# Moving two weight products ahead of the mask pooling in an eight-core masked linear and gated LoRA layer

## The reference

```python
xn = layernorm(x)
block_mask = mask.reshape(128, 32, 128, 32).sum(axis=(1, 3)) > 0      # 32 x 32 blocks of the int32 mask
s = einsum('bsk,nk->bsn', xn, weight * repeat(block_mask))            # 4096 x 4096
y = einsum('bth,oh->bto', xn, W_base) + b_base
z = einsum('bth,erh->bter', xn, lora_A[active])
alpha = softmax(log(domain_prior[active] + 1e-12) + logits(xn)[..., active])
y = y + einsum('bteo,bte->bto', einsum('bter,eor->bteo', z, lora_B[active]) * 2.0, alpha)
out = x + s * silu(y)
```

## Time and profile before

| | us |
|---|---|
| median of 3 runs | 2528.36 |
| lowest and highest run | 2517.14, 2659.54 |
| profiled execution, device time | 2527.91 |
| its span, slowest core (core 2) | 2526.2 |
| spans of the eight cores | 2501.1 to 2526.2 |
| iterations 0 to 20 of pass 0 | 367.4 to 1057.3 |
| iterations 21 to 31 of pass 0 | 1057.3 to 1366 |
| iterations of pass 1 | 1614 to 2520 |

### The profile page before, as it was taken

The page is one execution under the profiler, slowest core; times in us unless marked ns, Lnnn a source line. Parts: engine busy times, 40 slices in busy tenths (PEclk is TensorE's granted clock), DMA queues, the critical chain, the costliest instruction groups (busy, mean ns, idle before and its releaser), DMA issues.

```text
span 2526.2 us, 25213 instructions; the slowest of 8 cores (2501.1 to 2526.2 us)
## 1 busy us (share of the span) xinstructions
PE 2089.2 (83%) x8955; PEld 882.1 (35%) x8955; DVE 797.6 (32%) x871; ACT 469.2 (19%) x551; POOL 336.0 (13%) x260
## 2 busy tenths in 40 slices
PE   1135369889899898899998645699999999999998
PEld 0001024334344343344443101244444444444443
DVE  3631742444443344412221036322222122222221
ACT  2022001122111211222121320112211221122111
POOL 0123001111010111111012620010101010101010
PEclk9985579999999899999999556799999999999999
DMA  6853145667777676656563530256645665565552
GB/s 192 245 163 120 34 132 169 218 210 238 230 221 231 211 233 223 226 151 191 168 193 111 167 112 11 89 174 206 200 170 171 209 199 172 175 210 194 171 171 96
DMA packets 122834, 442.42 MB, mean 175 GB/s; under 512 B 15013, under 2 KB 15062, under 8 KB 122710
## 3 DMA queue, kind: packets, MB, share of 16 engines
q1 hardware_dynamic: 67414, 239.46, 30.2%
q10 hardware_dynamic: 46080, 167.79, 21.6%
q0 software_dynamic: 9216, 33.56, 3.3%
HBM read 407.17 MB, written 33.59 MB: 174 GB/s over the span
## 4 chain that ended last, share of the span: by engine, by line
PE 64%; DMA 16%; DVE 10%; issue 4%; POOL 3%; ACT 2%; SPq 1%; DVEq 0%; ACTq 0%; POOLq 0%
PE pb L741 30%; PE pb L761 29%; DMA mstage<-mkp 10%; DMA xbuf<-xt 3%; POOL sq L543 2%; DVE txn L612 2%; DVE xn L616 2%; DVE mcB L406 2%; DMA wstage<-wp 1%; DVE wm L498 1%; SPq L284 1%; PE pb L769 1%; DVE pooled L416 1%; PE pb L633 1%; DMA scr<-bm01a 1%
## 5 line engine op out<-in xcount | busy, mean ns | idle before, releaser
L741 PE MATMUL pb<-xn,wm 128*128 128x512 bf16 x4096 | 931.6, 387 | 48.1 <-DVE bm01a L435 48.1
L761 PE MATMUL pb<-xn,wb 128*128 128x512 bf16 x4096 | 904.9, 379 | 0.0
L741 PEld LDWEIGHTS pb<-xn,wm 128*128 128x128 bf16 x4096 | 405.5, 99 | 552.5 <-issue 89.9
L761 PEld LDWEIGHTS pb<-xn,wb 128*128 128x128 bf16 x4096 | 400.7, 98 | 483.4
L498 DVE TENSOR_TENSOR wm<-wstage,bmtexp 128x1024 bf16<-128x1024 f32 x256 | 342.8, 1339 | 646.4 <-DMA wstage<-wp 641.0
L797 POOL TENSOR_TENSOR out_sb<-sg_sb,xbuf 128x512 f32<-128x512 f32 x128 | 178.1, 1391 | 1932.2 <-DVE sg_sb L791 1932.2
L507 ACT CAST wb<-wbstage 128x1024 bf16<-128x1024 f32 x256 | 267.3, 1044 | 465.1 <-DMA wbstage<-wbp 461.9
L785 ACT ACTIVATE g_sb<-pb,b_sb 128x512 f32<-128x512 f32 x128 | 87.9, 687 | 1065.4 <-PE pb L769 651.3
L406 DVE TENSOR_TENSOR mcB<-mstage 128x512 bf16<-128x512 int32 x128 | 95.3, 744 | 407.9 <-DMA mstage<-mkp 403.0
L791 DVE TENSOR_TENSOR sg_sb<-pb,g_sb 128x512 f32<-128x512 f32 x128 | 87.7, 685 | 327.1 <-ACT g_sb L785 319.1
L543 POOL TENSOR_TENSOR sq<-xbuf 128x1024 bf16<-128x1024 f32 x64 | 121.0, 1892 | 213.2 <-DMA xbuf<-xt 150.0
(11 more groups left out here) (86 smaller groups left out, 338.9 us busy)
## 6 DMA issues: line engine op xcount, KB each, us to landing
wstage<-wp SPq DMA_DIRECT2D x256, 512.0 KB, 7.0
wbstage<-wbp ACTq DMA_DIRECT2D x256, 512.0 KB, 7.2
xbuf<-xt SPq DMA_DIRECT2D x128, 512.0 KB, 6.0
mstage<-mkp SPq DMA_DIRECT2D x64, 512.0 KB, 13.2
mstage<-mkp ACTq DMA_DIRECT2D x64, 512.0 KB, 6.4
out<-out_sb POOLq DMA_DIRECT2D x64, 512.0 KB, 9.4
wstage<-ap_ SPq DMA_DIRECT2D x4, 512.0 KB, 4.4
wbstage<-bp SPq DMA_DIRECT2D x4, 512.0 KB, 7.1
```

The costliest lines, as they stand in the source:

```text
L741: return e.matmul(pb[sbank][:], wm[i % 2][:, kc * 128:(kc + 1) * 128], xn[:, kc * TP + tb * TB: kc * TP + (tb + 1) * TB], start=(kc == 0), ...
L761: return e.matmul(pb[ybank][:], wb[i % 2][:, kc * 128:(kc + 1) * 128], xn[:, kc * TP + tb * TB: kc * TP + (tb + 1) * TB], start=(kc == 0), ...
```

## The change

In `plan_iter`, the calls that make products 0 and 1 and casts 0 and 1 for the next iteration and that issue the second half of the weights move from behind the first group of matmuls of the iteration to directly behind the issue of the first half, ahead of everything that concerns the mask band.

```diff
@@ -725,6 +725,9 @@
                 d_xt[(i + 1) * 128:(i + 2) * 128, p * TP:(p + 1) * TP],
                 writes=[f"xb{sl}"], tag=f"xr_p{p}i{i + 1}")
             w_loads_half(p, i + 1, 0)
+            wm_mults_half(p, i + 1, 0)
+            wb_casts_half(p, i + 1, 0)
+            w_loads_half(p, i + 1, 1)
 
         bj = i + 11
         if banding and i in (5, 13, 21):
@@ -748,10 +751,6 @@
                         tag=f"mms_p{p}i{i}t{tb}")
 
             if tb == 0:
-                if i + 1 < NN:
-                    wm_mults_half(p, i + 1, 0)
-                    wb_casts_half(p, i + 1, 0)
-                    w_loads_half(p, i + 1, 1)
                 if banding and bj <= 31:
                     band_mask_half(bj, 1)
 
```

## The result

The changed kernel is slower. Its median is 2591.82 us (10 runs, 2569.86 at the lowest), that of the kernel before 2528.71 us (10 runs); their ratio is 1.0216, with a 95% interval of 1.0179 to 1.0254, some 55 us. (Both medians also hold runs in which the cores of one die had a lower clock, up to 2827 us, which the ratio leaves out; this is why they differ by more than the ratio says.) The profiled execution took 2573.51 us, its slowest core, core 5, had a span of 2572.0 us. The forecast was 2537 us and the range ended at 2580: the median lies beyond it by 12 us, the median before times the ratio, 2583 us, by 3, and the profiled execution lies inside it.

The account below looks back on a forecast made before the run. It took a band iteration's period to be mask 0's landing plus VectorE's run behind it. 14.2 + 1.8 + 5.4 + 11.6 = 33.0 us against 32.57, +9 us together, gave 2537 us, range 2500 to 2580.

Parts of the forecast that it names:

- Landing of W quarter 1: In an iteration with a mask band, W quarter 1 lands at T+14.2 after the iteration's start T, against mean T+15.9.
- Product and issues: From W quarter 1's landing to mask 0's issue on SyncE: 1.8 us, 1.27 for a product and 0.5 for issuing.
- Mask 0's landing time: Mask 0, issued behind two W quarters on SyncE, takes 5.4 us to land; bounds 3.9 and 9.3.
- The sentence on the fit of 2.0 us plus bytes: One transfer takes 2.0 us plus bytes over 436 GB/s; by it mask 0 takes about 3.9 us, total 2510 us.
- VectorE's run from mask 0: From mask 0's landing to the next iteration's start, VectorE takes 11.6 us instead of 13.91, with mask 3 staying hidden.
- Iterations 5 and 13: Band iterations that end in the chain of e4l expansions; they get about half a microsecond each.
- Iterations 6 and 14: Costed at nothing: their masks on ScalarE's queue are late, so their cover is that queue, not SyncE's.
- Iteration 21: First iteration of pass 0 without a band; same queue order in both versions but for one 8 KB reload.
- the first: Late masks not paid back in band iterations: W quarter 1 stays at T+15.9, period 35.2 us, +48, 2576 us; chance 0.25.
- The second: Freed bandwidth in band iterations: W quarter 1 at T+12.3, mask 0 3.9 us, period 29.6, -52, 2476 us; chance 0.10.
- third: Mask work leaves the path in band iterations; TensorE sets the period at 28.3 us, -76, 2452 us; chance 0.03.
- The rule on early issue: Mask 0's landing moves by the whole 12.5 us of later issue: period 41.9, +169, 2697 us; chance 0.02.

Follow-up runs that it names:

- e3_late_masks: Kernel before, with masks 0 and 1 held on SyncE until W quarter 1 has landed, W quarters 2 and 3 behind them; 2562.31 us, ratio 1.0104.
- e1_vector_order: Changed kernel with only SyncE's order put back: masks 0 and 1 ahead of W quarters 2 and 3, products 0 and 1 still first on VectorE; 2525.12 us, ratio 0.9894.
- e4_masks_ahead: Kernel before, with masks 0 and 1 moved ahead of x for the next iteration on SyncE, VectorE as before; 2475.59 us, ratio 0.9716.
- e8_all_masks_ahead: Kernel before, with a fourth mask slot and all four masks issued by SyncE ahead of x, none by ScalarE; 2457.20 us, ratio 0.9680.
- e2_masks_between: Changed kernel with masks 0 and 1 one place earlier on SyncE, between W quarters 2 and 3; 2559.90 us, ratio 1.0080.
- e5_four_slots: Changed kernel with masks 0 and 1 back ahead of W quarters 2 and 3 on SyncE, plus a fourth mask slot; ratio 0.9883 to the kernel before.

## Why the prediction was wrong

It said no measurable change, 2537 us, and the kernel is slower by 2.2%, its median 12 us beyond the range. The structure of the sum held, and three of its four terms: a period is the landing of W quarter 1, a product and two issues, mask 0's landing time, and VectorE's run.

- *Landing of W quarter 1*: forecast T+14.2; in iteration 20, 1070.5 + 11.3 = 1081.8, T+14.3. Right, also in the mean of the 18 iterations (T+14.5). The reason given for it, that no masks follow, is not borne out: over all cores it is T+14.5 after T+14.9, and in e3_late_masks, where no mask follows at once either, it is T+15.3. The two iterations from which I took 11.2 us were a small sample.
- *Product and issues*: forecast 1.8 us; mask 0 issued at 1083.77, 2.0 us later. Right.
- *Mask 0's landing time*: forecast 5.4 us, measured 7.0 here, 6.7 in the mean of the 18 iterations, and 6.9 as the median of masks 0 and 1. **This is the step that failed.** In the prediction I took the middle of 4.9 us, the time of a W quarter with one transfer ahead of it, and of the startup's median. The queue has two W quarters ahead of the mask, and the runs show what they cost: 5.1 us with none (e3_late_masks), 6.0 us with two halves, 6.9 us with two wholes (mask 0 by itself, in the mean over all cores: 4.94, 5.35 and 6.69 us). The first burst was over by then: in iteration 20 the core's DMA engines moved only 11 GB/s from 1082 to 1085 us, in which the mask was issued. The nearest row should have been taken with one more transfer on top of it. The sentence on the fit of 2.0 us plus bytes, from the Trainium skill's "DMA: Bandwidth & Descriptors", section "Anatomy of one DMA", was further off still, 3.9 us: the section gives the fit for a single transfer on GpSimd's path, and these are issued by SyncE with others in flight. The least that the trace before has for a mask is 3.7 us (in the iterations with a band), not the 3.9 of the earlier trace rows.
- *VectorE's run from mask 0*: forecast 11.6 us, measured 11.65, and 11.8 in the mean. Right, and mask 3 stayed hidden, as forecast. e1_vector_order shows on how little that rests: with W quarters 2 and 3 in flight beside it mask 3 is late.
- *Iterations 5 and 13*: costed at half a microsecond each; they took 39.48 and 39.78 us, 3.5 and 2.0 more. The row that shows why is in the expansions of iteration 5:

```profile
567.46 0.21 PE L461 MATMUL pb<-bmra,e4l_sb 4*128 4x128 bf16 x1
571.23 0.47 PE L461 MATMUL pb<-bmra,e4l_sb 4*128 4x128 bf16 x2 [3.56 <-DVE bm01a L435]
```

The second expansion waits for the cast of line 435, and that stands behind products 2 and 3 on VectorE. The expansions start at the end of VectorE's run, not at that of the matmuls, so the whole delay of the first sum passes through, less the 2.2 us by which VectorE's run is shorter.

- *Iterations 6 and 14*: costed at nothing, though the 18 hold them: 35.2 after 31.0 us and 31.9 after 33.4, 2.7 together.
- *Iteration 21*: the reload that now stands behind W quarters 2 and 3 was costed at nothing; the iteration took 35.85 us after 33.4. In e1_vector_order, where the reload again stands ahead of them, it took 33.4.

Sum again with what was measured: 14.3 + 2.0 + 7.0 + 11.65 = 34.95 us, near the 35.05 of the mean. 45 us come from the 18 iterations, 5.6 from iterations 5 and 13, and 2.4 from iteration 21. The forecast was +9 us, and the spans differ by 45.8. Mask 0's term, 1.3 us too low in the mean, is worth 26 us over 20 iterations, most of what is missing; the rest is a few tenths in the other terms and the iterations costed at nothing.

Of the rivals, the first had the right price (35.2 us) and the right cause in the large, late masks that are not paid back, but got there by wrong terms: it left W quarter 1 at T+15.9 and gave the mask 5.9 us. Its chance of 0.10 beyond 2% was too small. Yet the period alone did not cross the line: 35.05 us is worth 2574 us by the prediction's own price. It took the few microseconds of iterations 5, 13 and 21 besides, and a timed difference (55 us) above that of the profiled spans (46), so that the range was missed narrowly. The second and third did not happen by this change, but e4_masks_ahead and e8_all_masks_ahead are what the third priced: 28.98 and 28.51 us against its 28.3. I had held that the mask work could not leave the path while products 2 and 3 stand behind it in VectorE's order; that was wrong. It leaves the path when the masks land early, with no change to VectorE's order. The rule on early issue ("Rules for kernel authors" on the same page) pointed the right way; the full price that I gave it, 12.5 us an iteration, was not paid, since a late mask lands in 6.9 us instead of 14.3.

What stays open: e2_masks_between, where a mask issued earlier took as long; e5_four_slots, where W quarter 1 and mask 0 landed earlier than in e1_vector_order; how the transfers in flight share the DMA engines was not taken apart further.

## What to carry to other kernels

A transfer that stands behind one that waits for a slot inherits its wait; before moving loads within a queue, write down for each what it will now stand behind, and what stands ahead of it in bytes when it is issued. Where the data an in-order engine needs first comes from a queue's tail, the gain is in issuing it before the stage's burst, in slots that are already free (here 3%), and not in reordering the engine's own work: with early masks the same reordering cost 1.9 us an iteration. And a price that no row shows, with the forecast near the edge of what it decides, deserves a chance as wide as its bounds.

## What the runs showed of the hardware

The same 512 KB of mask took 14.3 us to land as part of the first burst (iteration 12 before), and as the median of masks 0 and 1 over iterations 2 to 20 6.9 us behind two W quarters, 6.0 us behind two half ones, 5.1 us behind none. Issue time by itself says little: 12.8 us later at the issue were 5.5 us later at the landing (T+17.8 to T+23.3). That two masks behind it in the queue slow W quarter 1 is not shown: over all cores it landed at T+14.9 with them, and without them at T+14.5 in the changed kernel and at T+15.3 in e3_late_masks.
